# A two-layer graph kernel: one input on another DMA queue, its network's steps re-ordered between engines

## What is computed

```python
h = relu(layernorm(x))
x = x + Ahat @ (h @ w0) + bias          # layer 0; Ahat: 0/1 adjacency + eye, scaled by deg**-0.5 on both sides
h = relu(layernorm(x))                  # layer 1
s, v = (h @ w_in)[dst]                  # scalar and vector channels of each edge's node
W = (ssp(f @ W1 + b1) @ W2 + b2) * rcut # filter net on the edge inputs f (4352 x 20); ssp = softplus - log 2
agg = segment_sum(products(s, v, Yr, W), src)
x = x + output_net(agg)
```

## Time and profile before

| | |
|---|---|
| three runs, us | 71.66, 71.72, 71.74 (median 71.72) |
| the profiled execution, us | 71.83 |
| its span, us | 69.8 |
| busy, us: PE, PE weight load, DVE, ACT, POOL | 61.7, 48.6, 60.1, 48.6, 39.5 |
| chain that ended last, by engine | DVE 45%, PE 20%, ACT 13%, DMA 3% |

### The profile page before, as it was taken

One profiled execution on the slowest core, in us unless ns is written; L12 is line 12 of the kernel. 1 busy time (PEld: TensorE's weight loads), 2 busy tenths in 40 slices (PEclk: granted clock), 3 DMA queues, 4 the chain that ended last, 5 costly groups with the idle time before them and its releaser, 6 DMA issues.

```text
span 69.8 us, 1215 instructions
## 1 busy us (share of the span) xinstructions
PE 61.7 (88%) x407; PEld 48.6 (70%) x407; DVE 60.1 (86%) x124; ACT 48.6 (70%) x74; POOL 39.5 (57%) x46
## 2 busy tenths in 40 slices
PE   3999998999999999897998979999999999998340
PEld 1236754568834268796987969998898989997220
DVE  4599999999979968989999898989898999972760
ACT  0700059978999697967979999988696969732700
POOL 5000030000676989594799979999999988700000
PEclk9999999999999999999999999999999999999995
DMA  0899998984000000000000000000000000000044
GB/s 1 129 396 247 361 499 379 449 317 124 9 0 0 0 0 0 0 0 5 0 0 0 0 0 9 5 0 0 0 0 0 0 0 9 0 0 0 0 148 153
DMA packets 3049, 5.65 MB, mean 81 GB/s; under 512 B 540, under 2 KB 1936, under 8 KB 2916
## 3 DMA queue, kind: packets, MB, share of 16 engines
q1 hardware_dynamic: 2274, 5.14, 21.3%
q10 hardware_dynamic: 770, 0.44, 2.2%
HBM read 5.06 MB, written 0.52 MB: 80 GB/s over the span
## 4 chain that ended last, share of the span: by engine, by line
DVE 45%; PE 20%; issue 14%; ACT 13%; DMA 3%; DVEq 0%; ACTq 0%
ACT OsR L240 8%; DVE WQ L412 7%; DVE Os L412 7%; PE pair L632 5%; ACT w_sb L284 5%; DVE dst_bc L565 4%; PE pair L733 4%; PE pair L742 4%; DVE pair L514 3%; PE pair L674 3%; DMA idx_sb<-idx 3%; PE pair L721 3%; DVE w_sb L485 2%; DVE za L446 2%; DVE hX L449 2%
## 5 line engine op out<-in xcount | busy, mean ns | idle before, releaser
L733 PE MATMUL pair<-OsR,Mh 128*128 128x256 f32 x56 | 13.6, 281 | 0.0
L733 PE MATMUL pair<-OsR,Ml 128*128 128x256 f32 x56 | 13.6, 281 | 0.0
L721 PE MATMUL pair<-HL,OdT 128*128 128x256 f32 x68 | 10.1, 289 | 1.6 <-DVE dst_bc L565 0.7
L395 POOL TENSOR_TENSOR Ml<-dst_bc,Mh 128x512 fp32r<-128x512 f32 x8 | 10.4, 1305 | 1.1 <-ACT Mh L301 1.0
L721 PEld LDWEIGHTS pair<-HL,OdT 128*128 128x128 f32 x68 | 8.6, 188 | 2.8 <-issue 2.8
L733 PEld LDWEIGHTS pair<-OsR,Ml 128*128 128x128 f32 x56 | 10.5, 188 | 0.0
L733 PEld LDWEIGHTS pair<-OsR,Mh 128*128 128x128 f32 x56 | 10.5, 188 | 0.0
L605 PEld LDWEIGHTS pair<-WQ,Os 128*128 128x128 bf16 x68 | 6.8, 104 | 4.0 <-DVE WQ L412 1.8
L605 PE MATMUL pair<-WQ,Os 128*128 128x256 bf16 x68 | 9.4, 297 | 0.2 <-DVE WQ L412 0.2
L399 POOL TENSOR_TENSOR Ml<-dst_bc,Mh 128x512 fp32r<-128x512 f32 x7 | 9.2, 1309 | 0.0
L240 ACT ACTIVATE OsR<-Os 128x1024 fp32r<-128x1024 bf16 (+1 forms) x9 | 9.0, 999 | 0.0
(11 more groups left out here) (122 smaller groups left out, 140.2 us busy)
## 6 DMA issues: line engine op xcount, KB each, us to landing
dst_bc<-dst_row SPq DMA_DIRECT2D x1, 2176.0 KB, 12.9
w_sb<-w SPq DMA_DIRECT2D x1, 1024.0 KB, 8.1
x_sb<-x SPq DMA_DIRECT2D x1, 512.0 KB, 4.4
out<-x_sb SPq DMA_DIRECT2D x2, 192.0 KB, 1.9
f_sb<-f_t SPq DMA_DIRECT2D x1, 378.0 KB
b_sb<-bias SPq DMA_DIRECT2D x1, 256.0 KB, 13.1
w_sb<-w ACTq DMA_DIRECT2D x1, 128.0 KB, 4.1
out<-x_sb ACTq DMA_DIRECT2D x1, 128.0 KB, 1.9
```

Source lines behind the costliest of these rows:

```text
L395: nc.gpsimd.tensor_tensor(Ml[:, o, 0:n, feats(1)], M[:, o, 0:n, feats(1)], Mh[:, o, 0:n, feats(1)].bitcast(fp32), ALU.subtract).then_inc(q ...
L721: last = nc.tensor.matmul(gpair[g % 2][:, j * 2 * C:(j + 1) * 2 * C], OdT[:, a, t * P:(t + 1) * P], HL[:, a, :, :], start=(a == 0), stop=( ...
L733: last = nc.tensor.matmul(bank[4 + b][:, 0:N], part[:, g % RG, j, feats(b)], OsR[:, g % RG, j, :], start=(TG * g + j == 0 and part is Mh), ...
```

## The change

- The input f goes from the third place of SyncE's DMA queue to the third place of ScalarE's, behind w1 and w2.
- Waves: 2, 4, 6, 8, 8, 4, 2 tiles become 2, 2, 4, 4, 8, 8, 6. TensorE runs `hidden(0)` and `hidden(1)` behind tile 3 and `hidden(2)` behind tile 7, before behind tile 11.
- The first w0 step of node half 1 goes ahead of the transposes of `CI`. The four A products run with the node half outside.
- VectorE: `hX`'s remainder goes from before `CI` to behind the degrees, and with `hY`'s it is cut in three pieces; `xb` leaves VectorE; h2 also waits for `OdTa`.
- GpSimd: makes `xb`; b2 needs one subtraction (two fp32r parts on 64 rows in place of three bf16 parts on 96; the first part comes from ScalarE); it makes quarters 2 and 3 of `OdT` for `a` = 0 in a row, ahead of `s2`, and quarter 3 for `a` = 1 behind two `scaled_late`, with no wait for VectorE's quarters.
- ScalarE: b2's first part; `w2_hi` later; quarter 2 of `OdT` for `a` = 1 only, its two activations around `hW_hi`; `wc_sb` earlier.

```diff
-    WAVES = ((0, 2), (2, 6), (6, 12), (12, 20), (20, 28), (28, 32), (32, T))
+    TV = T
+    WAVES = ((0, 2), (2, 4), (4, 8), (8, 12), (12, 20), (20, 28), (28, TV))
...
         def _(sp):
             sp.dma_start(x_sb[:, :, :], x.rearrange("(a p) d -> p a d", p=P)).then_inc(d_x, 16)
-            sp.dma_start(f_sb[0:KF, :], f_t).then_inc(d_f, 16)
...
         def _(act):
             act.dma_start(w2_sb[:], w2).then_inc(d_w2, 16)
+            act.dma_start(f_sb[0:KF, :], f_t).then_inc(d_f, 16)
...
-            act.wait_ge(d_w2, 16)
-            nc.scalar.activation(w2_hi[:], w2_sb[:], ACT.Copy).then_inc(q["w2hi"], 1)
             act.wait_ge(q["zabs"], 3)
...
+            act.wait_ge(d_b2, 16)
+            nc.scalar.activation(b2p[:], b2_sb[:], ACT.Copy).then_inc(q["b2p"], 1)
+            act.wait_ge(d_w2, 16)
+            nc.scalar.activation(w2_hi[:], w2_sb[:], ACT.Copy).then_inc(q["w2hi"], 1)
...
-            pool.wait_ge(q["onehot"], len(WAVES))
-            pool.wait_ge(d_b2, 16)
-            nc.gpsimd.tensor_copy(b2p[:], b2_sb[:]).then_inc(q["b2p"], 1)
             pool.wait_ge(q["b2p"], 1)
+            nc.gpsimd.tensor_tensor(b2p[32:64, :], b2_sb[32:64, :], b2p[32:64, :].bitcast(fp32), ALU.subtract).then_inc(q["b2p"], 1)
...
+            pool.wait_ge(d_x, 16)
+            pool.wait_ge(d_b0, 16)
+            pool.wait_ge(q["z"], 3)
+            nc.gpsimd.tensor_tensor(xb[:, :, :], x_sb[:, :, :], b0_sb[:].unsqueeze(1).broadcast_to((P, NH, D)),
+                                    ALU.add).then_inc(q["xb"], 1)
...
-            node_onehots_late(3)
-            pool.wait_ge(q["OdTp"], 1)
+            node_onehots_late(0, 2)
+            node_onehots_late(0, 3)
+            pool.wait_ge(q["OdTp"], 2)
...
             scaled_late(1)
-            pool.wait_ge(q["OdT"], 4)
-            node_onehots_late(2)
+            node_onehots_late(1, 3)
             scaled_late(2)
...
-            dve.wait_ge(q["hhi"], 1)
-            nc.vector.tensor_tensor(hX[64:128, :], za[0:64, :], hX[0:64, :].bitcast(fp32), ALU.subtract).then_inc(q["hXlo"], 1)
+            dve.wait_ge(q["w2hi"], 1)
+            nc.vector.tensor_tensor(w2_lo[:], w2_sb[:], w2_hi[:].bitcast(fp32), ALU.subtract).then_inc(q["w2lo"], 1)
...
-            dve.wait_ge(d_b0, 16)
-            nc.vector.tensor_tensor(xb[:, :, :], x_sb[:, :, :], b0_sb[:].unsqueeze(1).broadcast_to((P, NH, D)),
-                                    ALU.add).then_inc(q["xb"], 1)
-            dve.wait_ge(q["hhi"], 2)
-            nc.vector.tensor_tensor(hY[0:64, :], za[64:128, :], hY[64:128, :].bitcast(fp32), ALU.subtract).then_inc(q["hYlo"], 1)
+            for c in range(3):
+                cols = slice(c * NG * P // 3, (c + 1) * NG * P // 3)
+                dve.wait_ge(q["hhi"], 1)
+                nc.vector.tensor_tensor(hX[64:128, cols], za[0:64, cols], hX[0:64, cols].bitcast(fp32),
+                                        ALU.subtract).then_inc(q["hXlo"], 1)
+            for c in range(3):
+                cols = slice(c * NG * P // 3, (c + 1) * NG * P // 3)
+                dve.wait_ge(q["hhi"], 2)
+                nc.vector.tensor_tensor(hY[0:64, cols], za[64:128, cols], hY[64:128, cols].bitcast(fp32),
+                                        ALU.subtract).then_inc(q["hYlo"], 1)
...
+            first_layer(1, 0, 1)
 
             pe.wait_ge(q["CI"], NH)
...
-            first_layer(1, 0, KD)
+            first_layer(1, 1, KD)
```

More of the change, by code:

```diff
@@ L240, in scatter_onehots @@
                 nc.scalar.activation(OsR[:, g % RG, 0:n, :], Os[:, t0:t0 + n, :], ACT.Copy).then_inc(q["OsR"], 1)
+            act.wait_ge(q["adj"], 1)
+            act.wait_ge(q["y"], 1)
+            y_blocks(0, free)
             act.wait_ge(d_dst, 16)
             act.wait_ge(q["negc"], 1)
[L244 to L247, removed]
+            act.wait_ge(q["tp1"], NH)
+            nc.scalar.activation(gap, dst_bc[:, E // 2:3 * E // 4], ACT.Abs, bias=iota_n[:, 1:2]).then_inc(q["gap"], 1)
             act.wait_ge(q["scales"], 1)
@@ L613, in hidden, with transposed @@
                 nc.tensor.matmul(zb[c][:, 0:hi - lo], w1_sb[:], f_sb[0:KF, lo:hi], start=True, stop=True).then_inc(q["z"], 1)
-            adjacency(range(2, 6))
-            adjacency(range(6, 12))
-            pe.wait_ge(d_f, 16)
-            pe.wait_ge(d_w1, 16)
-            for c in range(3):
-                hidden(c)
-            pe.wait_ge(q["eye"], NH + 1)
-            for a in range(NH):
+            def transposed(a):
+                pe.wait_ge(q["eye"], NH + 1)
                 pe.wait_ge(q["h1"], a + 1)
@@ L626, in _ @@
                 last.then_inc(q["tp1"], 1)
+            adjacency(range(2, 4))
+            pe.wait_ge(d_f, 16)
+            pe.wait_ge(d_w1, 16)
+            hidden(0)
+            hidden(1)
+            adjacency(range(4, 8))
+            hidden(2)
+            adjacency(range(8, 12))
+            transposed(0)
+            transposed(1)
             pe.wait_ge(d_w0, 16)
@@ L648, in filters @@
                 ps = fbank[g][:, 0:n * P]
-                nc.tensor.matmul(ps, ones[:], b2p[:].unsqueeze(1).broadcast_to((96, n, P)), start=True, stop=False)
+                nc.tensor.matmul(ps, ones[:], b2p[:].unsqueeze(1).broadcast_to((64, n, P)), start=True, stop=False)
                 for i, stack in enumerate((hX, hY)[0:n // 2]):
@@ L659, in _ @@
             first_layer(0, 2, 3)
[L660 removed]
+            adjacency(range(20, TV))
             first_layer(0, 3, KD)
+            first_layer(1, 0, 1)
             pe.wait_ge(q["CI"], NH)
@@ L667, in _ @@
             last.then_inc(q["CT"], 1)
-            first_layer(1, 0, KD)
-            for p, (part, ready) in enumerate(((hW_hi, "hW_hi"), (hW_lo, "hW_lo"))):
-                for b in range(NH):
+            first_layer(1, 1, KD)
+            for b in range(NH):
+                for p, (part, ready) in enumerate(((hW_hi, "hW_hi"), (hW_lo, "hW_lo"))):
                     pe.wait_ge(q[ready], b + 1)
```

67 lines of the change are left out of this document (31 added, 36 removed).

## The result

| | before | changed |
|---|---|---|
| runs beside each other, us (median) | 71.66 to 72.91 (71.73) | 83.0 to 83.6 (83.25) |
| profiled execution, us; its span | 71.83; 69.8 | 83.6; 81.5 |
| busy, us: PE, DVE, ACT, POOL | 61.7, 60.1, 48.6, 39.5 | 67.8, 61.5, 47.1, 42.3 |

The changed kernel takes 1.161 times as long (95% interval 1.158 to 1.164), 11.5 us more. The forecast was slower, at 77.9 us and at most 82.0: the side was right, the time is outside the range.

The account below looks back on a forecast made before the run. TensorE (88%) and VectorE (86%) were nearly full, so the price was the lateness of the edge loop's first sum: 1.6 + 1.75 + 2.85 = +6.2 us on 71.83, giving 78.0, as median 77.9 us; range 73.0 to 82.0.

Parts of the forecast that it names:

- Input f on ScalarE's queue, hidden layer after four tiles: TensorE's front: f lands at 7.2, h1's transposes start +0.85 us later (bounds 0 to +1.75), up to 1.5 more for the clock.
- Waves regrouped: Compares ahead of x's statistics: two more instructions, +0.12 us, hidden since TensorE is later than that.
- hX behind A, w0 step ahead of CI's transposes: TensorE after the adjacency: CI starts at 19.8, two w0 steps go before its transposes, which come at 21.45, +1.4 us.
- Six pieces, hW_lo: VectorE after the degrees: six subtractions of 0.45 us, hW_lo ends at 27.05, x1 starts at 27.9, +1.6 us.
- the new order of the A products: TensorE's A matmuls with b outside: worth nothing, as they wait for the last hW_lo.
- b2 in fp32r parts: b2's split: ScalarE loses about 2 us of work and is nowhere last; worth nothing.
- First collision: VectorE's h2, ready at 29.35, is held by GpSimd's second quarter until 31.15: 1.8 us later still.
- not later than needed: s2 on GpSimd follows sq1, so 30.53 becomes 33.9, without adding lateness.
- Second collision: GpSimd's unguarded third quarter holds VectorE's second pair of quarters, from 35.35 to 38.2: +2.85 us.
- Rival A: GpSimd holds two-source VectorE operations too; xb holds a last-wave compare until 18.8; 81.2 us, chance 0.32.
- My first check: First sign to look for in the changed profile: the hidden layer on TensorE starts near 7.2.

## Why the prediction was wrong

- **"Input f on ScalarE's queue, hidden layer after four tiles" is the step that failed.** I took 7.2 for the landing, by b2's row, and +0.85 in sum, with +1.75 as its far end and up to 1.5 more for the clock. Measured: 9.80, and +6.97. Two things were wrong in it. b2 is 48 KB, and f is 378 KB and had to share the engines with w0; it is no row to price f by (behind f, in the changed kernel, b2's own 32 KB took 9.8 us, and its 48 KB took 11.0 in the run with f's queue alone, not 5.6). And the clock's price was put as an aside: the pause kept TensorE at half level not for the passes alone but until 16.7 us, over four long passes and 16 matmuls. At h1's transposes the two parts cost 1.4 and 3.95 us alone and 6.97 together, in the traces.
- *Waves regrouped, +0.12 hidden*: right; x's statistics began at 6.65 against 6.64, with the first compare 0.12 us earlier (2.90 against 3.02).
- *hX behind A, w0 step ahead of CI's transposes*: of my +1.4, 0.7 was the step's own; measured 0.5.
- *Six pieces, hW_lo, +1.6*: 0.2 beyond the transposes of CI by my working, 0.6 measured. The pieces do shorten the pows (2.00 for 2.94), as said. That the new order of the A products is worth nothing was not tested.
- *b2 in fp32r parts, nothing*: wrong. 1.7 us alone, 0.7 to 0.8 on the chain ahead of h2's transposes. I priced b2's split on GpSimd and ScalarE and never asked what its matmul costs on TensorE.
- *First collision, +1.8*: did not happen. h2 took 0.49 us in the middle of the second quarter. s2's place in GpSimd's queue, which the forecast passed over as "not later than needed", is what counts in the kernel before; here it was hidden.
- *Second collision, +2.85*: happened, at 0.9.
- *Rival A, chance 0.32*: its first half was right and decided 1.5 us: xb holds a compare of VectorE. It put that at 18.8 beside an undisturbed front. The Trainium skill, SBUF — State Buffer, section "SBUF: two separate sides", has the loser of the port pair blocked for the whole instruction; for xb the rows agree (2.35 us on GpSimd, a compare 1.66 us longer, 2.15 alone), for the quarters they don't (3 us on GpSimd, holds of 0.7 to 1.0, and h2's square, with two SBUF inputs, was done 1.3 us before the quarter beside it).
- My first check, "the hidden layer starts near 7.2", was the right one to name, and failed at once.

In sum I had x1 late by 1.6 us and 4.6 us arising behind it. Measured: 9.6 us late at x1, and 1.7 us between x1 and the first sum. So the two errors go opposite ways, 8.0 us too little ahead of x1 and 2.9 too much behind it, and without the second the forecast would have been further off. I looked for the price where GpSimd and VectorE meet, and it lay in the first ten microseconds.

## What to carry to other kernels

Before an input changes its queue, ask what it will share the engines with, not what stands ahead of it in the queue: take the row of a transfer of its own size. Before TensorE is made to wait early in a kernel, ask what the wait does to its clock: here the passes behind it ran at half speed, and independent work ahead of the wait (even useless work) brought 2.3 us back. And two edits that each cost nothing to undo alone may share a cover; undo them together before calling them free.
